# Last dense layer: a chunk of one node tile first, then six of four, with the next chunks' node work between the units

## The chip, the cores and the metric

The kernel runs on one core of one Trainium2 chip. The metric is device time in microseconds (us). Engines: PE is TensorE's matrix multiply and PEld its weight load, DVE is VectorE, ACT is ScalarE, POOL is GpSimd, SP is SyncE, which here only issues DMAs.

## The reference, cut to what matters

Two blocks of graph layer and feed-forward layer run over 3125 nodes of 256 features. The change touches the front of the last feed-forward layer, on the output x of the second graph layer:

```python
# second graph layer: weighted sums over edges, a head's sum divided by its denominator
attn = ex / jnp.maximum(denom[dst], 1e-10)
out = jax.ops.segment_sum(h_src * attn[..., None], dst, num_segments=n)
return out.reshape(n, H * D) + bias
...
# last layer, on the normalized x
H = jax.nn.gelu(xf @ W1 + b1, approximate=False)          # 256 -> 1024
probs = jax.nn.softmax((H @ Wg + bg) / TEMP, axis=-1)     # 8 experts
assign = jnp.argmax(probs, axis=-1)
out = sum over e of where(assign == e, probs[:, e] * (H @ Wd[e] + bd[e]), 0)
...
x = x + _L1_ffn_ref(_layernorm(x, axis=-1)[None], ...)[0]
```

## The kernel before

The 3125 nodes are 25 tiles of 128. Most of the 2.4 ms is spent in stages before the one that is changed: planning and ordering the edges, two graph layers, the first feed-forward layer. Stages are blocks of code one behind the other; every engine has an instruction list of its own in each block, engines wait for one another by semaphores, and a block ends for all engines when the last of them, SP among them, is through.

The change is in `hidden1`, the block that makes the hidden units H of the last layer and the gate's logits. The block behind it routes the nodes to experts, and the one behind that (`last_experts`) gathers rows of H from a table in DRAM (`htab`) and multiplies them with each expert's weights.

`hidden1` goes over the tiles in chunks of CT = 4: six of four tiles and then one of one tile, 128 columns wide instead of 512. A chunk c has FC1 = 8 units j = 8c + f of 128 hidden features each. What each engine does:

- DVE, `node(i)` (lines 1898 to 1904): four operations on a tile: sums times reciprocal of the denominator, plus bias, added to x, and the statistics of the row. `norm.variance(c)` (lines 930 to 936) makes the variances of a chunk in seven small operations, one after the other. `normalized(c)` takes the reciprocal of the root and writes the normalized tiles (line 949). `units_back(j)` (line 1918) copies a unit that was transposed back from PSUM into the buffer `hr`.
- PE, `turn(i)` (line 1955): transposes a normalized tile, in two halves, through two PSUM buffers; `hidden(j)` (line 1965): the matrix product of a unit; `turn_units(j)` (line 1975): transposes the unit back, a tile at a time; `gates(r)` (line 1984): the gate's product over four units; `back(c)` (line 1991): the gate's result turned back.
- ACT, `norm.root(c)` (line 941): the square root; `copy_turned(i)` (line 2023): a transposed tile from PSUM to SBUF; `units(j)` (line 2031): the gelu; `flips(c)` (line 2037): the gate's result from PSUM. Sqrt and gelu need different activation tables, so a root between gelus stands between two table loads, which the profile shows as ACT_TABLE_LOAD on the line of the activation they are for.
- SP: at first the layer's weights, then W1's inputs ahead of 8 MB of expert weights `w2`; then for each chunk x and the units to `htab`, half a chunk's units in one DMA (`store_units`, line 1879).

The order is written out by hand. On DVE, all node work of chunks 0 and 1 stands ahead of the first unit; after that, chunk c + 2's nodes stand between chunk c's units. On ACT, the roots of chunks 0 and 1 both stand ahead of the copies of chunk 0's tiles. PE transposes tile f - 3 of chunk c + 1 behind `hidden` of unit f, from f = 3 on. The waits that tie the engines:

- `hidden(j)` waits for all copies of its chunk's tiles and, as its PSUM has two buffers, for the gelu of unit j - 2;
- `turn_units(j)`, which stands behind `hidden(j + 1)`, waits for the gelu of unit j and, having two buffers too, for `units_back(j - 2)`;
- `turn(i)` waits for the normalized tile i and for the copy of tile i - 2;
- PE's first instruction of the block (line 1996) waits for W1, the biases and the gate's weights.

Of the kernel before, what the change touches and what calls it, by code (L numbers as in the profile page):

```python
# [11 lines left out]
P = 128  # L12
# [3 lines left out]
NT = (N + P - 1) // P  # L16
# [14 lines left out]
FC0, FC1 = F0 // P, F1 // P  # L31
# [849 lines left out]
TB = 5  # L881
# [29 lines left out]
class Norm:  # L911

    def __init__(self, a, tag, per=None):
        self.per = per or TB
        self.st = a.sb(f"{tag}_st", [P, NT, 6])
        self.mean, self.var, self.t0 = (a.sb(f"{tag}_{m}", [P, NT]) for m in ("mean", "var", "t0"))
        self.s_var, self.s_std = a.sem(f"{tag}_var"), a.sem(f"{tag}_std")

    def of(self, c):
        return slice(c * self.per, min(c * self.per + self.per, NT))

# [896 lines left out]
CT = 4  # L1820
CTURNS = (NT + CT - 1) // CT


def hidden1(nc, a, cst, A, x, acc, front):
# [18 lines left out]
    p_g, p_l = a.ps("p_g", [P, 512]), a.ps("p_l", [P, 512])  # L1843
    norm = Norm(a, "norm", CT)
    s_chain, s_in, s_b1, s_bt, s_n, s_t, s_xt, s_h, s_ht, s_g, s_flip, s_l = (a.sem(m) for m in (
# [4 lines left out]
    def tiles(c):  # L1850
        return range(c * CT, min(c * CT + CT, NT))

    def wide(c):
        return len(tiles(c)) * P

    with nc.Block() as block:

        @block.sync
        def _(sp):
# [22 lines left out]
            store_x(0)  # L1882
            store_x(1)
            for c in range(CTURNS):
                store_units(2 * c)
                store_units(2 * c + 1)
                if c + 2 < CTURNS:
                    store_x(c + 2)
            sp.wait_ge(s_store, 16 * CTURNS)
# [4 lines left out]
        def _(dve):  # L1894
# [31 lines left out]
            dve.wait_ge(s_bi, 16)  # L1926
            for c in two:
                for i in tiles(c):
                    node(i)
                norm.variance(link, V, c)  # L1930
                normalized(c)
            for j in range(CTURNS * FC1):
                c, f = j // FC1, j % FC1
                units_back(j)
                if c + 2 < CTURNS:
                    if f < len(tiles(c + 2)):
                        node(tiles(c + 2)[f])
                    if f == CT:
                        norm.variance(link, V, c + 2)
                    if f == CT + 2:  # L1940
                        normalized(c + 2)
            dve.wait_ge(s_in, 64)
            dve.wait_ge(s_l, CTURNS)
# [3 lines left out]
        def _(pe):  # L1947
            T = nc.tensor

            def turn(i):  # L1950
# [3 lines left out]
                for k in range(KC):  # L1954
                    last = T.transpose(p_t[i % 2][:, k * P:(k + 1) * P], n[i // CT % 2][:, i % CT, k * P:(k + 1) * P],
                                       cst["ident"][:])
# [42 lines left out]
            for j in range(CTURNS * FC1):  # L1999
                c, f = j // FC1, j % FC1  # L2000
                hidden(j)
                if c + 1 < CTURNS and f >= 3 and f - 3 < len(tiles(c + 1)):
                    turn(tiles(c + 1)[f - 3])
                if j:
                    turn_units(j - 1)
                if j and j % WAYS == 0:
                    gates(j // WAYS - 1)
                if c and f == 2:
                    back(c - 1)
# [5 lines left out]
        def _(act):  # L2015
            S = nc.scalar

            def copy_turned(i):
                c, b = i // CT, i % CT
                act.wait_ge(s_t, i + 1)  # L2020
# [21 lines left out]
            norm.root(act, S, 0)  # L2042
            norm.root(act, S, 1)
            for i in tiles(0):
                copy_turned(i)
            for j in range(CTURNS * FC1):
                c, f = j // FC1, j % FC1
                units(j)
                if c and f == 0:
                    flips(c - 1)  # L2050
                if f == CT + 2 and c + 2 < CTURNS:
                    norm.root(act, S, c + 2)
                if c + 1 < CTURNS and f >= 3 and f - 3 < len(tiles(c + 1)):
                    copy_turned(tiles(c + 1)[f - 3])
            flips(CTURNS - 1)
# [465 lines left out]
```

## Time and profile before

| | us |
|---|---|
| median of 3 runs | 2420.26 (2420.16, 2420.26, 2425.25) |
| span of the profiled execution, first to last instruction | 2421.0 |
| PE busy, whole span | 1785.6 (74%) |
| DVE busy, whole span | 1638.0 (68%) |
| ACT busy, whole span | 805.9 (33%) |
| `hidden1` in the span, about | 2076 to 2243 |

The profiled execution's own time is known by its span alone; the span is 0.7 us above the median of the runs. A busy share over the whole span says little about one block; the rows further down are from `hidden1` alone, but for two, and their times count from the span's start.

### The profile page before, as it was taken

To read this page: it belongs to the slowest core of one execution; us is meant where nothing else is said; L and a number is where in the kernel's file an instruction comes from. 1 tells how busy PE (TensorE), PEld (TensorE's weight loads), DVE (VectorE), ACT (ScalarE), POOL (GpSimd) and SP (SyncE) were. 2 spreads that over 40 slices of the span, in tenths; PEclk is the share of its full clock that TensorE was granted. 3 is DMA by queue.
4 is the path that set the end of the run, shared out by engine and by line. 5 is a ranking of instruction groups with operands and counts; after the bars stand their busy time and mean duration, and the time that the engine had idled before them with its cause. 6 is when DMAs were issued, how large, how long until landed. Compare 5 with 4: busy or idle time off the path is not lost. (4 is left out here: it accounts for less than half of the span.)

```text
span 2421.0 us, 41392 instructions
## 1 busy us (share of the span) xinstructions
PE 1785.6 (74%) x11452; PEld 1386.4 (57%) x11452; DVE 1638.0 (68%) x3379; ACT 805.9 (33%) x2077; POOL 1152.8 (48%) x1106
## 2 busy tenths in 40 slices
PE   3466666655179996399992878888887887499598
PEld 1245445544057775299991546666665665255587
DVE  8655565555167778655556849999999999764443
ACT  7433333322000002333331644444444444244221
POOL 0277777777700000055550057777777776000243
PEclk9677887887589999599996889999999999799799
DMA  3355555544388862522225145555555553533353
GB/s 86 110 190 192 188 189 173 172 167 165 128 298 284 294 216 103 200 64 73 71 68 180 39 146 146 145 150 142 151 152 145 145 144 113 194 131 119 123 180 104
DMA packets 203758, 368.03 MB, mean 152 GB/s; under 512 B 63193, under 2 KB 111162, under 8 KB 203159
## 3 DMA queue, kind: packets, MB, share of 16 engines
q1 hardware_dynamic: 148066, 205.99, 26.2%
q0 software_dynamic: 54624, 159.35, 21.3%
q8 instruction: 106, 1.74, 0.3%
q14 instruction: 112, 0.92, 0.1%
q10 hardware_dynamic: 850, 0.04, 0.0%
HBM read 235.32 MB, written 130.87 MB: 151 GB/s over the span
## 5 line engine op out<-in xcount | busy, mean ns | idle before, releaser
L2136 POOL DMA_INDIRECT att_rows<-hdram,top_ix x440 | 502.8, 1143 | 264.0 <-issue 133.8
L874 POOL DMA_INDIRECT mtab<-first_w,msgs_ix x280 | 277.5, 991 | 85.3 <-issue 81.1
L1177 POOL IOTA route_spare<- 128x65 f32 (+1 forms) x2 | 0.4, 177 | 522.3 <-POOLq L1115 522.3
L2217 PE MATMUL att_p_acc<-att_msg,att_hot 128*128 128x264 f32 x880 | 225.8, 401 | 14.7 <-DVE wts_wn L2396 6.5
L736 PE MATMUL msgs_p_m<-nodes_n,msgs_hott 128*128 x592 | 185.1, 467 | 48.8 <-issue 30.7
L2251 ACT ACTIVATE att_enc<-att_p_z 128x1024 f32<-128x1024 f32 x110 | 112.7, 1024 | 308.8 <-PE att_p_z L2157 308.8
L2217 PEld LDWEIGHTS att_p_acc<-att_msg,att_hot 128*128 128x128 f32 x880 | 163.4, 196 | 53.2 <-issue 26.6
L874 POOL DMA_INDIRECT mtab<-msgs_rw,msgs_ix x160 | 160.6, 1004 | 68.9 <-issue 44.8
L2166 PE MATMUL att_p_h<-heads_parts,att_hz 128*128 x1320 | 184.3, 295 | 1.4 <-DVE att_enc L2323 1.4
L637 DVE TENSOR_TENSOR first_w<-msgs_p_m,msgs_sorted 128x1024 f32<-128x1024 f32 x70 | 85.6, 1223 | 140.3 <-PE msgs_p_m L736 113.1
L736 PEld LDWEIGHTS msgs_p_m<-nodes_n,msgs_hott 128*128 128x128 f32 x592 | 132.4, 235 | 76.7 <-issue 56.0
L2166 PEld LDWEIGHTS att_p_h<-heads_parts,att_hz 128*128 128x128 bf16 x1320 | 138.2, 105 | 55.0 <-issue 18.2
L2323 DVE TENSOR_TENSOR att_enc<-att_enc,att_p_h 128x1024 f32<-128x1024 f32 x110 | 133.7, 1215 | 20.6 <-PE att_p_h L2166 20.5
L772 PE MATMUL msgs_p_m<-first_w,msgs_hott 128*128 128x256 f32 x616 | 143.2, 385 | 1.2 <-issue 0.3
L2379 DVE TENSOR_TENSOR att_msg<-att_rows,att_ex 128x1024 f32<-128x1024 f32 x110 | 134.7, 1225 | 3.7
L2325 DVE TENSOR_REDUCE att_al<-att_enc 128x32 f32<-128x1024 f32 x110 | 134.2, 1220 | 3.8
L2157 PE MATMUL att_p_z<-top_ewz,att_hz 128*128 128x512 bf16 x220 | 70.5, 403 | 82.7 <-issue 78.5
L1371 PEld LDWEIGHTS exp_hidden<-exp_xt,exp_own 128*128 128x128 f32 x1040 | 127.8, 194 | 4.5 <-issue 1.2
L772 PE MATMUL msgs_p_m<-msgs_rw,msgs_hott 128*128 128x256 f32 x360 | 86.7, 394 | 58.4 <-issue 58.0
L772 PEld LDWEIGHTS msgs_p_m<-first_w,msgs_hott 128*128 128x128 f32 x616 | 110.9, 189 | 32.3 <-issue 17.2
L1371 PE MATMUL exp_hidden<-exp_xt,exp_own 128*128 128x128 f32 x1040 | 128.3, 277 | 1.0 <-DVE exp_own L1317 1.0
L1381 PE MATMUL exp_y<-exp_own,exp_ht 128*128 128x256 f32 x520 | 123.1, 380 | 0.9 <-issue 0.9
(408 smaller groups left out, 3811.7 us busy)
## 6 DMA issues: line engine op xcount, KB each, us to landing
first_w<-mtab SPq DMA_DIRECT2D x77, 520.0 KB, 4.6
etab<-msgs_et SPq DMA_DIRECT2D x110, 288.0 KB, 2.5
att_hz<-etab SPq DMA_DIRECT2D x110, 288.0 KB, 2.9
msgs_rw<-mtab SPq DMA_DIRECT2D x45, 520.0 KB, 4.7
htab<-hid_hr SPq DMA_DIRECT2D x12, 1024.0 KB, 4.3
first_w<-in_L_ffn_w SPq DMA_DIRECT2D x16, 512.0 KB, 5.0
ffn0x_w<-in_L_ffn_w SPq DMA_DIRECT2D x16, 512.0 KB
ffn_w<-in_L_ffn_Wd SPq DMA_DIRECT2D x8, 1024.0 KB
```

The costliest lines, as they stand in the source:

```text
L736: last = T.matmul(p_m[g % 2][:, q, :], hott[g % AHEAD][:, q, :], node[q // UQ], start=True, stop=True)
L772: last = T.matmul(p_m[g % 2][:, 0, :], hott[g % 2][:, q, :], rw[g % RS][:, q, 0:C], start=(q == 0), stop=(q == G - 1))
L874: nc.gpsimd.indirect_dma_start(mtab, bass.IndirectOffsetOnAxis(ap=ix[:, g, q:q + 1], axis=0), rw[g % RS][:, q, :], None).then_inc(s_free[g ...
L1371: last = T.matmul(hidden[t % 2][:, f * P:(f + 1) * P], own1[:, k, f * P:(f + 1) * P], xt[t % 2][:, k * P:(k + 1) * P], start=(k == 0), sto ...
L1381: last = T.matmul(y[t % 2][:, 0:C], ht[t % 2][:, f, :], own2[:, f, :], start=(f == 0), stop=(f == FC - 1))
L2136: nc.gpsimd.indirect_dma_start(rows[:, g % RS, q, :], None, hdram, bass.IndirectOffsetOnAxis(ap=ix1[:, g, q:q + 1], axis=0)).then_inc(s_ro ...
L2166: last = T.matmul(p_h[:, q, :], hott_of(g, q), own[g][q // UQ][:, k, H:HN], start=(k == 0), stop=(k == 2))
L2217: last = T.matmul(p_acc[u % 2][:, 0:HW], hot[g % 2][:, q, :], msg[g % 2][:, q, :], start=(r == 0), stop=(r == UQ - 1))
L2251: S.activation(enc[g % 2][:], p_z[:], ACT.Relu).then_inc(s_enc, 1)
L2323: V.tensor_tensor(e[:], e[:], p_h[:], ALU.mult).then_inc(s_prod, 1)
L2325: V.tensor_reduce(al[t % 2][:, j * G:(j + 1) * G, :].rearrange("p q h -> p (q h)"), e[:].rearrange("p q (h d) -> p (q h) d", h=H), AX, ALU ...
L2379: V.tensor_tensor(msg[g % 2][:].rearrange("p q (h d) -> p q h d", d=D + 1)[:, :, :, 0:D], rows[:, g % RS, :, 0:C].rearrange("p q (h d) -> ...
```

## The change

- The chunks are now bounded by `LEAD` = 0, 1, 5, 9, ..., 25: first one of one tile, then six of four. `Norm` takes these bounds.
- DVE: ahead of the first unit stands only tile 0's node work. Chunk 1's four nodes stand behind units 0 to 3 of chunk 0, its variance behind unit 3, its normalization behind unit 4. Behind every unit of chunk 1 stands a node of chunk 2 or, from unit 4, of chunk 3; chunk 2's variance behind unit 3 and its normalization behind unit 4; chunk 3's variance behind unit 7, its normalization behind unit 1 of chunk 2. From chunk 2 on, as before.
- ACT: `root(1)` and `root(2)` behind the fifth gelu (f = 4) of chunks 0 and 1, `root(3)` behind the second gelu of chunk 2.
- PE: chunk 1's four tiles are transposed behind unit 7 of chunk 0; chunk 2's tiles two and two behind `hidden` of units 6 and 7 of chunk 1; later ones as before.
- SP: x of chunk c + 1, not c + 2, is stored behind chunk c's units; only chunk 0's x ahead of them.

```diff
-    def __init__(self, a, tag, per=None):
-        self.per = per or TB
+    def __init__(self, a, tag, per=None, starts=None):
+        per = per or TB
+        self.starts = starts or [*range(0, NT, per), NT]
...
-        return slice(c * self.per, min(c * self.per + self.per, NT))
+        return slice(self.starts[c], self.starts[c + 1])
...
-CTURNS = (NT + CT - 1) // CT
+LEAD = [0, *range((NT - 1) % CT + 1, NT + 1, CT)]
+CTURNS = len(LEAD) - 1
...
-    norm = Norm(a, "norm", CT)
+    norm = Norm(a, "norm", starts=LEAD)
+    chunk_of = [c for c in range(CTURNS) for _ in range(LEAD[c + 1] - LEAD[c])]
...
-        return range(c * CT, min(c * CT + CT, NT))
+        return range(LEAD[c], LEAD[c + 1])
...
+    def turned_at(c, f):
+        if c + 1 == CTURNS:
+            return ()
+        if c == 0:
+            return tiles(1) if f == FC1 - 1 else ()
+        if c == 1:
+            return {FC1 - 2: tiles(2)[:CT // 2], FC1 - 1: tiles(2)[CT // 2:]}.get(f, ())
+        return tiles(c + 1)[f - 3:f - 2] if f >= 3 else ()
...
             store_x(0)
-            store_x(1)
             for c in range(CTURNS):
                 store_units(2 * c)
                 store_units(2 * c + 1)
-                if c + 2 < CTURNS:
-                    store_x(c + 2)
+                if c + 1 < CTURNS:
+                    store_x(c + 1)
...
-            for c in two:
-                for i in tiles(c):
-                    node(i)
-                norm.variance(link, V, c)
-                normalized(c)
+            for i in tiles(0):
+                node(i)
+            norm.variance(link, V, 0)
+            normalized(0)
             for j in range(CTURNS * FC1):
                 c, f = j // FC1, j % FC1
                 units_back(j)
-                if c + 2 < CTURNS:
+                if c < 2:
+                    if f < CT:
+                        node(tiles(c + 1)[f])
+                    elif c == 1:
+                        node(tiles(c + 2)[f - CT])
+                    if f == CT - 1:
+                        norm.variance(link, V, c + 1)
+                    if f == CT:
+                        normalized(c + 1)
+                    if c == 1 and f == FC1 - 1:
+                        norm.variance(link, V, c + 2)
+                elif c + 2 < CTURNS:
...
+                if c == 2 and f == 1:
+                    normalized(c + 1)
...
                 hidden(j)
-                if c + 1 < CTURNS and f >= 3 and f - 3 < len(tiles(c + 1)):
-                    turn(tiles(c + 1)[f - 3])
+                if c:
+                    for i in turned_at(c, f):
+                        turn(i)
                 if j:
                     turn_units(j - 1)
                 if j and j % WAYS == 0:
                     gates(j // WAYS - 1)
+                if c == 0:
+                    for i in turned_at(c, f):
+                        turn(i)
...
             norm.root(act, S, 0)
-            norm.root(act, S, 1)
             for i in tiles(0):
                 copy_turned(i)
...
-                if f == CT + 2 and c + 2 < CTURNS:
+                if c < 2 and f == CT:
+                    norm.root(act, S, c + 1)
+                if c == 2 and f == 1:
+                    norm.root(act, S, c + 1)
+                if c >= 2 and f == CT + 2 and c + 2 < CTURNS:
                     norm.root(act, S, c + 2)
-                if c + 1 < CTURNS and f >= 3 and f - 3 < len(tiles(c + 1)):
-                    copy_turned(tiles(c + 1)[f - 3])
+                for i in turned_at(c, f):
+                    copy_turned(i)
```

## Rows read from the trace of the kernel before

**Rows 1.** Windows: length; busy us of PE, PEld, DVE, ACT, POOL; clock; DMA share, GB/s.

```profile
2076.00:2103.00 27.00, 2.82 (x10) 1.95 (x11) 21.47 (x63) 3.55 (x9) 0.00 (x0) 0.52 0.97 323
...
2125.00:2232.00 107.00, 106.91 (x475) 55.50 (x474) 58.59 (x143) 46.81 (x76) 0.00 (x0) 1.00 0.33 120
```

**Rows 2.** Timeline, first 30 us: start, us, engine, line, operation [idle before].

```profile
2085.34 0.24 PE L1996 MATMUL hid_p_l<-top_ident,hid_flat 8*128 8x8 f32 x1 [11.78 <-DMA hid_bg<-in_L_ffn_bg]
...
2088.68 1.28 ACT L941 ACT_TABLE_LOAD   x1 [2.90 <-DVE hid_norm_var L936]
...
2100.47 0.20 ACT L941 ACTIVATE hid_norm_t<-hid_norm_var 128x4 f32<-128x4 f32 x1 [10.29 <-DVE hid_norm_var L936]
...
2101.07 1.09 PE L1955 MATMUL hid_p_t<-top_ident,hid_n 128*128 128x128 f32 x4 [9.07 <-ACT hid_xt L2023]
...
2101.77 0.80 ACT L2023 COPY hid_xt<-hid_p_t 128x256 f32<-128x256 f32 x2 [0.57 <-PE hid_p_t L1955]
...
2102.62 6.35 PE L1965 MATMUL hid_p_h<-hid_xt,hid_w 128*128 128x512 f32 x8 [0.46 <-ACT hid_xt L2023]
...
2106.44 0.69 ACT L2031 ACTIVATE hid_ht<-hid_p_h,hid_b1t 128x512 f32<-128x512 f32 x1 [2.57 <-PE hid_p_h L1965]
```

**Rows 3.** Timeline of DVE in the first wide chunk: units with nodes, variance, normalization.

```profile
2109.45 0.69 DVE L1918 COPY hid_hr<-hid_p_r 128x512 f32<-128x512 f32 x1 [7.15 <-PE hid_p_r L1975]
...
2111.89 0.69 DVE L1918 COPY hid_hr<-hid_p_r 128x512 f32<-128x512 f32 x1
...
2120.60 0.15 DVE L930 TENSOR_TENSOR hid_norm_mean<-hid_norm_st 128x4 f32<-128x4 f32 x1
...
2121.79 0.16 DVE L936 SCALAR_TENSOR_TENSOR hid_norm_var<-hid_norm_var,hid_norm_t 128x4 f32<-128x4 f32 x1
...
2125.26 1.38 DVE L949 TENSOR_SCALAR hid_n<-top_x,hid_norm_mean,hid_norm_t 128x256 f32<-128x256 f32 x4
```

**Rows 4.** Timeline of PE: first unit of the second chunk, fourth unit, last wide unit.

```profile
2124.25 1.89 PE L1965 MATMUL hid_p_h<-hid_xt,hid_w 128*128 128x512 f32 x4
...
2132.97 1.96 PE L1965 MATMUL hid_p_h<-hid_xt,hid_w 128*128 128x512 f32 x4
...
2229.64 1.88 PE L1965 MATMUL hid_p_h<-hid_xt,hid_w 128*128 128x512 f32 x4
```

**Rows 5.** Timeline, end of the block: narrow units, gate, first operation behind the block.

```profile
2232.45 0.37 ACT L2031 ACTIVATE hid_ht<-hid_p_h,hid_b1t 128x128 f32<-128x128 f32 x1 [0.20 <-PE hid_p_h L1965]
...
2232.99 0.69 DVE L1918 COPY hid_hr<-hid_p_r 128x512 f32<-128x512 f32 x1 [0.30 <-PE hid_p_r L1975]
...
2240.57 0.29 DVE L1918 COPY hid_hr<-hid_p_r 128x128 f32<-128x128 f32 x1 [0.39 <-PE hid_p_r L1975]
...
2241.28 0.39 PE L1991 MATMUL hid_p_l<-hid_pick,hid_flip 128*128 128x8 f32 x2 [0.39 <-ACT hid_flip L2037]
...
2243.52 0.17 DVE L1120 TENSOR_SCALAR gate_rev<-top_iota 128x8 f32<-128x8 f32 x1 [1.38 <-PEq L1856]
```

**Rows 6.** Waits of SP's queue: who waited for whom: us, times, longest.

```profile
SPq L1891 <- DMA htab<-hid_hr: 1.7, 1, 1.7
```

**Rows 7.** DMA issues of the block: operation, count, KB each, median us to landing.

```profile
htab<-hid_hr SPq DMA_DIRECT2D x12, 1024.0 KB, 4.3
```

**Rows 8.** Timeline of ACT: table loads and their waits, an earlier block and this one.

```profile
1285.49 1.28 ACT L941 ACT_TABLE_LOAD   x1
1303.78 0.21 ACT L941 ACTIVATE upd_norm_t<-upd_norm_var 128x5 f32<-128x5 f32 x1 [17.00 <-DVE upd_norm_var L936]
...
2122.34 1.28 ACT L941 ACT_TABLE_LOAD   x1
...
2124.12 1.28 ACT L2031 ACT_TABLE_LOAD   x1
```

**Rows 9.** Windows: the clock's rise at the start, its fall behind the block.

```profile
2105.00:2110.00 5.00, 5.00 (x12) 2.20 (x11) 0.55 (x1) 1.37 (x2) 0.00 (x0) 0.70 1.04 389
...
2244.00:2246.00 2.00, 0.00 (x0) 0.00 (x0) 1.73 (x6) 0.83 (x2) 0.00 (x0) 0.63 0.01 4
```

More of the change, by code:

```diff
@@ L1954, in turn @@
                 for k in range(KC):
-                    last = T.transpose(p_t[i % 2][:, k * P:(k + 1) * P], n[i // CT % 2][:, i % CT, k * P:(k + 1) * P],
+                    last = T.transpose(p_t[i % 2][:, k * P:(k + 1) * P], n[chunk_of[i] % 2][:, i - LEAD[chunk_of[i]], k * P:(k + 1) * P],
                                        cst["ident"][:])
@@ L2018, in copy_turned @@
             def copy_turned(i):
-                c, b = i // CT, i % CT
+                c, b = chunk_of[i], i - LEAD[chunk_of[i]]
                 act.wait_ge(s_t, i + 1)
```

## The prediction

> **What bounds the kernel now.** The chain that ended last holds only the final store, so it says nothing of this block. The windows by stretch do. Up to 2103 PE works 2.8 of 27 us while DVE works 21.5: a head bound by DVE. From 2125 to 2232 PE is busy 106.9 of 107 us, so PE alone sets the pace of the wide chunks [rows 1]. The timeline of the head shows why it lasts: ACT's second root waited 10.3 us for chunk 1's variance, and the copies of chunk 0's tiles, queued behind it, held PE back until the first `hidden` at 2102.62 [rows 2]. At the other end the last matmul is over at 2241.67, the last unit's copy at 2240.86; SP then waits 1.7 us for the last store to land, and the next block's first DVE operation stands at 2243.52 [rows 5, 6]. So the store of the last units ends the block. From the start of the last wide `hidden`, 2229.64, to this release are 13.88 us [rows 4, 5]. The change shortens the head's first wait, and in exchange puts DVE's nodes on PE's way in chunks 0 and 1. So I sum four places: when the first wide `hidden` starts, what chunks 1 and 2 lose against before's wide chunks, and the tail.
>
> **First narrow unit.** Three nodes fewer stand ahead of chunk 0's variance, so that is no longer last: ACT comes free at 2085.78 (2088.68 less its idle 2.90), behind the loads that PE awaited until 2085.34 [rows 2]. From there: table load 1.28, root 0.2, reciprocal and first normalization 0.6 (a quarter of 1.38, and two short steps), transposes to copy 0.73, copy 0.4 [rows 2, 3]: `hidden(0)` at 2089.2, 13.4 us before its like.
>
> **Chunk 0.** The clock is at half there: a wide `hidden` took 3.4 us plus 0.4 to its gelu (2102.62 to 2106.44), a narrow one then a quarter, 0.85, plus 0.4 [rows 2]. With gelu 0.37 [rows 5] and 0.5 for the transposes back, DVE starts at 2091.35. Here PE, ACT and DVE don't share equally: a wide unit with its node took DVE 2.44 us, without idle between [rows 3]; a narrow copy is 0.40 shorter (0.29 for 0.69 [rows 5]), so 2.04. Four of them and the variance, 1.35 from its first to the end of its seventh operation [rows 3], end at 2100.9. Behind it hang ACT's root and, behind that in ACT's list, the table load and gelu 5, and PE behind gelu 5.
>
> Is the load for the root also on this chain? In an earlier block the load stands right behind ACT's last work, 17 us before its variance came [rows 8]; at 2088.68 it stood behind its variance [rows 2]. In the code the first root waits for one semaphore, the other for two; the moved roots wait for one, so I take the first and keep 1.28 for the range. Then: root 0.25, load 1.28, gelu 0.37, `turn_units(5)` and `hidden(7)` 1.5, gelu 7 0.37 (2104.7). Chunk 1's four tiles now pass two PSUM buffers one behind the other; the last copy ends 2.2 later (0.73 and 0.4 a pair, begun while gelu 7 ran). First wide `hidden`: 2106.9, so **4.3 us later** than before (2102.62). The 13.4 us won are spent.
>
> **Chunk 1.** PE idles from about 2097 to 2102.9, so I start it at half clock. Before, the clock rose at 2108.0 (0.70 as the mean of 2105 to 2110 [rows 9]), 6.9 us after the transposes at 2101.07 [rows 2]; about as long from 2102.9 is 3.0 us into chunk 1. Counted from its first `hidden`: that takes 3.2, narrow transposes and gate 0.45, the second `hidden` 1.7, transposes and hop 0.65: first copy back at 6.0. A node stands behind every unit, so DVE's list in this chunk sums to 8 x 2.44 + 2 x 1.35 + 1.6 = 23.8 [rows 3], against the 21.6 that PE took for a wide chunk. Four units, variance, one more unit with its node, reciprocal and first normalization: 9.76 + 1.35 + 2.44 + 0.6 bring the first tile of chunk 2 at 20.2. PE got there at about 17.3 (five units from 5.35 on, at 1.7 for a product, half of the 3.4 above, and a sixteenth of that, 0.11, for each of the four transposes, with a gate's 1.0 and hops 0.3), and stands 2.9 us. `root(2)` with its load back is over by 18.7 and is hidden behind this. Then two transposes, `turn_units`, `hidden`, two more and `turn_units` (3.6), and 0.75 until the last two copies, which stand behind gelu 7: 24.55. Before's first wide chunk took 2124.25 - 2102.62 = 21.63, half clock included [rows 2, 4]: **2.9 us lost**.
>
> **Chunk 2.** Chunk 1's last unit reaches DVE behind chunk 2's first `hidden`, at 24.55 + 1.7 + 0.65 = 26.9; with its node and chunk 3's variance DVE is through at 30.7. Two units with nodes, 4.88, and 0.6 bring chunk 3's first tile at 36.2. PE wants it behind its fourth `hidden`, 24.55 + 8.72 + 1.7 = 35.0 (8.72 from 2124.25 to 2132.97 [rows 4]): **1.2 us lost**, with 0.3 and 2 as ends. Its pair of loads is hidden as it is in unit 6 of every wide chunk now.
>
> **Nothing for the rest.** The number of roots among wide chunks is as before, five; PE's list there has one transposed tile less, 0.24. SP's stores of x moved behind units wait for tiles long done, and `store_units` behind them go out when their copies end; the expert weights' queue only delays the first of them, whose buffer is wanted again 20 us later.
>
> **Tail.** The last chunk is wide. Last `hidden` to the end of its copy: 2233.68 - 2229.64 = 4.04 [rows 4, 5]; its store is 1 MB, 4.3 to landing [rows 7]; release 0.6 later (2243.52 less 2240.86, less the wait of 1.7 and about 0.4 for the issue): 8.94 instead of 13.88, **4.94 us won**. The gate's end, by 6.6, is covered by the store; were the store as quick as the last one was, the gate would end the block and 2 us more be won.
>
> **Sum.** 4.3 + 2.9 + 1.2 - 0.24 - 4.94 = +3.2 us. It is made on the profiled execution, whose span, 2421.0, lies 0.7 above the median; I add it to the median: 2423.5.
>
> The Trainium skill (ScalarE: Activation LUTs, What ACT_TABLE_LOAD costs) gives a switch about 1.28 us and as much again of drain, 2.66 in all. Here the load agrees, but between the loads at 2122.34 and 2124.12 only 0.5 us is left for a root and a copy [rows 8], so no drain is seen. By the page the load back in chunk 0 would cost 1.38 more, and the sum be +4.6.
>
> **Rivals.**
> - *Clock up early.* If PE's work on narrow units lets the clock rise before chunk 1, that starts DVE's row 1.4 us sooner and the sum is +1.8, 2422.0. For it: PE works most of the last 4 us ahead. Against: a 5 us idle before.
> - *Clock falls again.* PE's 2.9 us stand in chunk 1 may put it back to half: it fell at 2244.5 (0.63 as mean of 2244 to 2246 [rows 9]), 2.8 us after the last matmul [rows 5]. The next rise costs half of 5.4 us, as 2102.62 to 2108.0 did: +5.9, 2426.2. The Trainium skill (TensorE: Matmul & The Clock Gate, HAM oscillation) has such gaps in a loop put the clock back each time; the fall in the row agrees with it.
> - *The load stands behind its wait*, as at 2088.68: 1.28 more in chunk 0, some 0.5 in chunk 1: +5.0, 2425.3.
> - *A switch costs a second load's 1.28*, in ACT's list where no idle is shown: on the chain once, +4.5, 2424.8.
> - *Faster.* Chunk 1's nodes fit between narrow units. Before, the eight narrow units at the end went through in some 9 us. At that pace the first wide `hidden` is at 2089.2 + 9 + 2.2 = 2100.4, 2.2 sooner than before, and with DVE ahead chunks 1 and 2 lose nothing: -2.2 - 0.24 - 4.94 = -7.4, 2412.9. It decides for faster where the first three terms together are under 0.3. Against it: DVE had no idle between units with nodes [rows 3], and a narrow unit saves it only 0.40.
>
> **How the numbers follow.** Forecast 0.52; clock early 0.17; clock falls 0.17; load behind its wait 0.04; dearer switch 0.03; faster 0.07. 0.2%, about what a measurement of this kernel can tell from no change, is 4.8 us, so the forecast with its spread (2.0 to 4.8) and the early clock lie within it. Slower: the fall 0.17, half of the two small cases, and 0.06 of the forecast's upper end: 0.27. Faster 0.07, the same 0.66. The low end of the range is the early clock with chunk 2's loss at 0.3: +0.9, and a little under it for hops that I priced too high: 2420.5. The high end is the fall with the clock's first rise late too (1.2 more): 2427.5.
>
> **What would show it.** First `hidden` at 2089 and first wide `hidden` at 2106.9 (2100 for the faster rival); in chunk 0 DVE without idle from 2091 to 2101, ACT's root(1) right behind variance 1, its load ahead of it. In chunk 1 PE waiting for DVE's line 949, some 3 us, and again, shorter, in chunk 2. PE idle ahead of the first wide `hidden` while ACT copies. At the end SP's wait for the last store some 4 us, ended by its landing. A first wide `hidden` off by over 2 us, no wait on line 949, or a store that lands in 2 us would make the sum wrong.

## The result and the profile after

The changed kernel took 2433.38 us (median of 20 runs, 2424.87 to 2439.81) beside 2424.91 for the kernel before (20 runs, 2417.36 to 2436.26): a ratio of 1.0036, 95% interval 1.0025 to 1.0047; of 2424.91 that is 8.7 us more, with 6.1 and 11.4 as ends (the two medians themselves lie 8.5 apart). The prediction was 2423.5 with 2427.5 as its upper end. The three runs of before that it was added to had a median of 2420.26, which lies 4.65 below that of the 20.

The profiled execution of the changed kernel has a span of 2438.0, 17.0 more than the one of before. Most of that is not in the block that was changed: its first DVE operation stands at 2089.01 instead of 2076.50. From there to the release of the next block are 170.89 us instead of 167.02, and from the release (the next block's first DVE operation) to the end 178.07 instead of 177.43. Below, the block is also counted from PE's first matmul in it, since what stands ahead of that is the wait for the weights, 7.9 to 9.2 us in the profiles of the two kernels: 161.72 instead of 158.18.

The head and the first two chunks, in the timeline of the changed kernel (start, us, engine, line, operation, idle before):

```profile
2098.18 0.24 PE L2019 MATMUL hid_p_l<-top_ident,hid_flat 8*128 8x8 f32 x1 [12.12 <-DMA hid_bg<-in_L_ffn_bg]
...
2101.99 2.08 PE L1988 MATMUL hid_p_h<-hid_xt,hid_w 128*128 128x128 f32 x8 [0.46 <-ACT hid_xt L2050]
...
2104.32 0.29 DVE L1929 COPY hid_hr<-hid_p_r 128x128 f32<-128x128 f32 x1 [3.54 <-PE hid_p_r L1998]
...
2106.88 1.28 ACT L942 ACT_TABLE_LOAD   x1
...
2113.89 0.21 ACT L942 ACTIVATE hid_norm_t<-hid_norm_var 128x4 f32<-128x4 f32 x1 [5.72 <-DVE hid_norm_var L937]
2114.11 1.28 ACT L2058 ACT_TABLE_LOAD   x1
...
2115.83 0.47 PE L1998 MATMUL hid_p_r<-top_ident,hid_ht 128*128 128x128 f32 x1 [6.19 <-ACT hid_ht L2058]
...
2119.80 1.98 PE L1988 MATMUL hid_p_h<-hid_xt,hid_w 128*128 128x512 f32 x4 [0.46 <-ACT hid_xt L2050]
...
2138.81 0.76 PE L1978 MATMUL hid_p_t<-top_ident,hid_n 128*128 128x128 f32 x4 [2.46 <-DVE hid_n L950]
...
2140.09 3.33 PE L1988 MATMUL hid_p_h<-hid_xt,hid_w 128*128 128x512 f32 x4
...
2144.74 1.98 PE L1988 MATMUL hid_p_h<-hid_xt,hid_w 128*128 128x512 f32 x4 [0.44 <-ACT hid_xt L2050]
...
2156.55 0.44 PE L1978 MATMUL hid_p_t<-top_ident,hid_n 128*128 128x128 f32 x2 [1.28 <-DVE hid_n L950]
```

These answer to [rows 2, 3]. Counted from PE's first matmul (2098.18), the first `hidden` is 3.81 us behind it (17.28 before), the first wide one 21.62 (4.3 later than before). ACT's second root waits 5.72 us for its variance, with its table already loaded; PE stands (sits idle between two pieces of work) 6.19 us for the gelu that is queued behind. In chunk 1, from 2119.80 to 2144.74, PE stands 2.46 us for DVE's normalized tile, and the `hidden` behind this stand takes 3.33 us, the one ahead of it and the others 1.9 to 2.0. In chunk 2 it stands 1.28 us for DVE. The same two chunks as windows (length, busy us of PE, PEld, DVE, ACT, POOL, clock, DMA share, GB/s):

```profile
2119.80:2144.74 24.94, 22.04 (x88) 11.01 (x88) 17.10 (x44) 9.55 (x16) 0.00 (x0) 0.93 0.27 98
2144.74:2167.73 22.99, 21.71 (x96) 11.36 (x97) 18.58 (x51) 10.94 (x18) 0.00 (x0) 1.00 0.32 115
```

The clock was full (2.4 GHz) when chunk 1 began and fell to half (1.2 GHz) in the stand, so that its mean is 0.93; before, it was low at the start of the first wide chunk [rows 9] and full in all later ones [rows 1]. The end of the block, and the wait of SP's queue in it:

```profile
2251.03 1.88 PE L1988 MATMUL hid_p_h<-hid_xt,hid_w 128*128 128x512 f32 x4
...
2255.10 0.36 SPq L1891 DMA_DIRECT2D htab<-hid_hr  x1
...
2259.90 0.17 DVE L1121 TENSOR_SCALAR gate_rev<-top_iota 128x8 f32<-128x8 f32 x1 [2.32 <-PEq L1868]
```

```profile
SPq L1902 <- DMA htab<-hid_hr: 3.8, 1, 3.8
```

Against [rows 5, 6]: the last wide `hidden` starts 8.87 us ahead of the release, not 13.88, and the wait for the last store has grown from 1.7 to 3.8.

### The profile page after: what moved, and what is told of

Read it like the earlier page. It is cut to its first block and busy times, and to the rows that moved or that the text cites. A ratio compares the mean times of both kernels' runs of the same rounds, so it can differ in the third digit from the quotient of the medians.

```text
span 2438.0 us, 41398 instructions
## 1 busy us (share of the span) xinstructions
PE 1796.6 (74%) x11452; PEld 1395.8 (57%) x11452; DVE 1640.4 (67%) x3379; ACT 809.0 (33%) x2079; POOL 1158.1 (48%) x1106
## 5 line engine op out<-in xcount | busy, mean ns | idle before, releaser
L2247 PE MATMUL att_p_acc<-att_msg,att_hot 128*128 128x264 f32 x880 | 231.6, 409 | 13.9 <-DVE att_total L2423 6.5
```

The costliest lines, as they stand in the source:

```text
L2247: last = T.matmul(p_acc[u % 2][:, 0:HW], hot[g % 2][:, q, :], msg[g % 2][:, q, :], start=(r == 0), stop=(r == UQ - 1))
```

## The experiments

**First group: drift or the change?** Three theories stood against each other for the 17 us between the two profiles: (A) the change costs what its block shows, the rest is drift of the stages ahead; (B) the changed program also lengthens the stages ahead; (C) the block itself costs about 8 in most runs.

*The changed kernel, run again.* No edit.

> The changed kernel as it is, timed and profiled once more. Theory A (the change costs what its block shows, about 4 us, and the rest of the 8.5 us is run-to-run drift of the stages ahead): block from PE's first matmul to the next block's first DVE operation 161 to 162.5 us against 158.2 before, and the whole time 3 to 6 us above the kernel before in this job. Theory B (the change also lengthens the stages ahead, by where the program lies): block as in A, the whole time 8 us above or more, and the first matmul of the block again some 8 to 13 us later than before's 2085.3. Theory C (the block itself costs about 8 us in most runs, and the profiled run was lucky with the clock): block 165 us or more.

Measured: 2429.37 (12 runs), ratio 1.0030 [1.0013, 1.0046], which is 7.3 us (3.2 to 11.1): more than A's 3 to 6, less than B's 8, with an interval that holds both. In its profile the block begins at 2073.24, 3.3 us sooner than in the kernel before, and takes 161.79 from the first matmul, as A and B have it. So C falls, and the 12.5 us ahead of the block do not come with the change each time. They did not come from the attention stage alone either: 6.0 of them were there when its first transfer started, first in the kernel before, then in the changed one:

```profile
1408.47 0.32 SPq L2124 DMA_DIRECT2D att_seg<-segtab  x1
```

```profile
1414.47 0.32 SPq L2154 DMA_DIRECT2D att_seg<-segtab  x1
```

A smaller part of B is not excluded. From that transfer to the block's first DVE operation the three full profiles of the changed kernel take 674.5, 669.6 and 671.9 us, those of the kernel before 668.0, 667.9 and, with the padding below, 670.4: 3.2 more on the mean, with ranges that overlap.

*Both kernels without the attention stage:*

```
-                with ExitStack() as c1:
-                    attention(nc, Pool_(nc, c1, "att"), ...
```

> The kernel before without the second graph layer's attention stage, so that the sums keep the values they are started with. That stage is the one whose gathers make times drift. It takes about 690 us of the span, so 1720 to 1740 us is expected by all theories; what tells them apart is its difference to the next kernel.

> The changed kernel without the attention stage, to be compared with the one above. A: 3 to 5 us longer, all of it between the block's first matmul and the next block. B: as much in the block, and 2 us or more in the stages ahead of it. C: about 8 us longer, all in the block.

Measured: 1753.81 and 1760.07 (5 runs each), 6.26 apart. Block 165.25 and 171.16, 5.9 apart, which is nearly all of it. The difference is over A's 3 to 5 and under C's 8. The block begins 6.0 us later in the changed kernel's profile (1410.77 against 1404.80), as B has it, but that profile is of the slowest of its five runs and the other of the fastest, so it settles nothing. That the attention stage is the one that drifts is borne out in part at most: it took 666.1 to 674.5 us in the full profiles, but without it five runs of one kernel still spread over 8.6 us. That its gathers are the cause no run shows.

*The kernel before with a few instructions more* at the end of the block:

```
+            for k in range(4):
+                link(V.memset(pad[:, k:k + 1], 0.0))
...
+            for k in range(2):
+                S.copy(pad[:, 4 + k:5 + k], b1t[:, k:k + 1])
```

> The kernel before with four tiny DVE operations and two tiny ACT copies at the end of the block, as many instructions as the change adds on these engines, where both engines wait. A and C: the same as the kernel before, within 2 us, and the block 158 to 159 us. B: 3 us or more slower, in the stages ahead of the block.

Measured: ratio 0.9998 [0.9982, 1.0013]; block 165.71, from the first matmul 157.32 (expected 158 to 159). These instructions cost nothing that can be told within some 4 us either way, so B's 3 us or more is not seen.

**Second group: the change taken apart.** The first theory of each expectation is the one of the block's own terms.

*The normalization ahead of the node,* in chunks 0 and 1 of the changed kernel:

```
                 if c < 2:
+                    if f == CT:
+                        normalized(c + 1)
                     if f < CT:
                         node(tiles(c + 1)[f])
...
-                    if f == CT:
-                        normalized(c + 1)
```

> The changed kernel, but in chunks 0 and 1 the normalizations of the next chunk stand on DVE ahead of the node behind the fifth unit, not behind it. Theory 1 (chunk 1 is long because PE stands 2.46 us for DVE's first normalization, and because the clock falls in that stand, 3.33 us instead of 1.88 for the hidden behind it): the node took 1.7 us of that path, so PE's stand in chunk 1 is about 0.7 us, the clock stays up, chunk 1 takes 22 to 23 us instead of 24.93, the first wide hidden starts some 0.5 us earlier or as before, and the kernel is 2 to 3 us faster than the changed one: ratio about 1.002 to the kernel before. Rival (the clock falls for another reason than this stand, or DVE's row as a whole is the bound): chunk 1 stays at 24 to 25 us and the ratio at 1.003 to 1.004.

Measured: 2423.74, ratio 1.0006 [0.9994, 1.0018]. PE's timeline:

```profile
2102.76 3.78 PE L1988 MATMUL hid_p_h<-hid_xt,hid_w 128*128 128x512 f32 x4 [0.46 <-ACT hid_xt L2050]
...
2121.84 0.76 PE L1978 MATMUL hid_p_t<-top_ident,hid_n 128*128 128x128 f32 x4 [0.62 <-DVE hid_n L950]
...
2123.43 1.88 PE L1988 MATMUL hid_p_h<-hid_xt,hid_w 128*128 128x512 f32 x4
```

The stand is 0.62 as expected and the `hidden` behind it takes 1.88: no fall. But here the clock was still at half when chunk 1 began (3.78 for its first `hidden`), so the chunk lasts 23.86 us, not 22 to 23. The median is better than expected (1.5 us over before, -1.5 to 4.4), the block, 170.27, worse: one profile of a kernel does not stand for its runs where the clock is in play, and the attention stage took 666.1 us in this one, less than in any other.

*Only the chunk bounds,* with the order of the kernel before (cut to the bounds themselves):

```
-CTURNS = (NT + CT - 1) // CT
+LEAD = [0, *range((NT - 1) % CT + 1, NT + 1, CT)]
+CTURNS = len(LEAD) - 1
```

> Only the chunk bounds are changed (1 tile and six times 4), the order of the work is that of the kernel before. Theory 1 (the loss in chunks 1 and 2 comes from the nodes between the units, the gain at the end from the wide last chunk): chunks 1 and 2 lose nothing against a wide chunk but the late rise of the clock, the tail still takes 8.9 us, and the last stage is as in the kernel before. The first hidden waits for chunk 1's nodes and stands some 13 us behind the first matmul, the first wide hidden some 23.5 us, 2 us later than in the changed kernel: block 168 to 169 us, total 1 to 3 us over the kernel before. Rival (the narrow chunk itself makes the losses): chunk 1 takes 24 us and more here too, the block 171 us or more, total 5 us over or more.

Measured: 2424.11, ratio 1.0009 [0.9998, 1.0020]; block 168.96. Timeline of ACT and PE:

```profile
2095.23 0.21 ACT L942 ACTIVATE hid_norm_t<-hid_norm_var 128x4 f32<-128x4 f32 x1 [9.32 <-DVE hid_norm_var L937]
...
2095.75 2.07 PE L1968 MATMUL hid_p_h<-hid_xt,hid_w 128*128 128x128 f32 x8 [8.45 <-ACT hid_xt L2026]
...
2106.66 0.30 PE L1978 MATMUL hid_p_r<-top_ident,hid_ht 128*128 128x128 f32 x1 [1.23 <-DVE hid_hr L1921]
...
2108.35 3.78 PE L1968 MATMUL hid_p_h<-hid_xt,hid_w 128*128 128x512 f32 x4 [1.40 <-ACT hid_xt L2026]
```

The root of chunk 1 holds the head for 9.32 us, as before, and narrow units wait for DVE: the first wide `hidden` comes 24.40 behind the first matmul. The chunk behind takes 22.72 (clock at half at first), the next 21.65, a wide chunk's time, and the last `hidden` starts 9.00 ahead of the release. So the losses of chunks 1 and 2 come from the new order, and the gain at the end from the bounds. That it is the nodes in this order rather than the root or the transposes rests on PE's waits for DVE and on the swap above, which took 1.84 us off the stand by moving one node.

*Only the nodes and the root between the units* (and the transposes that hang on them), with the bounds of the kernel before:

```
-            for c in two:
+            for i in tiles(0):
+                node(i)
...
+                if c < 1:
+                    if f < CT:
+                        node(tiles(c + 1)[f])
+                    else:
+                        node(tiles(c + 2)[f - CT])
...
-            norm.root(act, S, 1)
...
+                if c < 1 and f == CT:
+                    norm.root(act, S, c + 1)
```

> Bounds as in the kernel before (six times 4 and 1); only the nodes, variance, normalizations and root of chunk 1 stand between the units of chunk 0, as the changed kernel has them in its chunk 1. Theory 1 (the nodes between the units cost what they push back: about 3 us in the first chunk and 1.3 in the next, but let the first hidden start some 9 us sooner): first hidden at 8 us behind the first matmul instead of 17, chunk 0 24 to 25.5 us instead of 21.6, the chunk behind it 1.3 longer, total 3 to 5 us faster than the kernel before. Rival (wherever nodes stand between units, the first chunk runs at half clock and stands for DVE, and the gain at the head is spent again): total within 2 us of the kernel before.

Measured: 2419.34, ratio 0.9980 [0.9964, 0.9995]. PE's timeline:

```profile
2092.35 5.83 PE L1986 MATMUL hid_p_h<-hid_xt,hid_w 128*128 128x512 f32 x8 [0.46 <-ACT hid_xt L2044]
...
2112.80 0.76 PE L1976 MATMUL hid_p_t<-top_ident,hid_n 128*128 128x128 f32 x4 [2.65 <-DVE hid_n L950]
...
2113.93 3.49 PE L1986 MATMUL hid_p_h<-hid_xt,hid_w 128*128 128x512 f32 x4
```

The first `hidden` is 8.59 behind the first matmul, 8.7 sooner than in [rows 2]; the first chunk takes 26.37, not 24 to 25.5, with such a stand (2.65) and such a fall of the clock (3.49) as in the changed kernel. By the runs about half of the 8.7 us is left (4.8, with 1.2 and 8.7 as ends), as theory 1 had it. The profile shows less: the release is 155.57 behind the first matmul, 2.6 sooner than in the first profile of before, and the stage behind it takes 179.8, the longest of all.

*Only ACT's root of chunk 1 moved,* behind the second gelu:

```
             norm.root(act, S, 0)
-            norm.root(act, S, 1)
...
+                if j == 1:
+                    norm.root(act, S, 1)
```

> The kernel before with one thing moved: ACT's root of chunk 1 stands behind the second gelu instead of ahead of the copies of chunk 0's tiles. Theory 1 (the head of the block before was held back by this root's wait of 10.3 us alone): the first hidden starts about 8 us behind the first matmul instead of 17, DVE still does chunk 1's nodes first, and PE stands for the first unit back or not at all: block 6 to 8 us shorter, total 5 to 8 us faster. Rival (DVE's 24 nodes bound the head, whatever the order on ACT): the first wide chunk becomes longer by as much as the head becomes shorter, total within 2 us.

Measured: 2413.63, ratio 0.9969 [0.9952, 0.9986]; block 158.59. Timeline:

```profile
2088.30 6.01 PE L1965 MATMUL hid_p_h<-hid_xt,hid_w 128*128 128x512 f32 x8 [0.46 <-ACT hid_xt L2023]
...
2095.06 1.28 ACT L941 ACT_TABLE_LOAD   x1
...
2096.36 0.20 ACT L941 ACTIVATE hid_norm_t<-hid_norm_var 128x4 f32<-128x4 f32 x1
...
2098.11 0.68 DVE L1918 COPY hid_hr<-hid_p_r 128x512 f32<-128x512 f32 x1
```

The first `hidden` is 7.69 behind the first matmul, and DVE does all nodes of chunk 1 (four, of the eight at the head) while PE transposes and works on the first two wide units, mostly at half clock. The root waits for nothing, PE is busy 21.71 us of this chunk's 22.07, and the release is 149.28 behind the first matmul, 8.1 sooner than on the mean of before's profiles below. In PE's waits of the block's first 50 us the one for a normalized tile is that of the first transposes (us, times, longest):

```profile
PE hid_p_t L1955 <- DVE hid_n L949: 4.7, 1, 4.7
```

**Third group: the clock, and what one profile is worth.**

*The changed kernel with its stands filled* by matmuls that nothing reads:

```
+                for k in range({FC1 - 2: 16, 2 * FC1 - 2: 8}.get(j, 0)):
+                    T.matmul(p_l[:, 256:512], cst["ident"][:], w1[:, 0, 0:256], start=True, stop=True)
```

> The changed kernel, with matmuls that nothing reads put into PE's list where it stands: 16 of 256 columns ahead of the transposes of unit 5 in chunk 0 (PE stands 6.2 us there), 8 ahead of chunk 2's first transposed tile in chunk 1 (2.5 us there). Theory 1 (the stand of 2.46 us in chunk 1 put the clock back to half, and the hidden behind it took 3.33 us instead of 1.88): with the fillers the clock stays up from chunk 0 on, chunk 1's first hidden and the one behind the stand both take 1.9 to 2.0 us, chunk 1 lasts 23.4 us instead of 24.93, and the block is 1.4 us shorter than the changed kernel's 170.9 if the fillers fit into the stands. Rival (the fall has another cause, or DVE's row sets the end of chunk 1 anyway): chunk 1 stays within 0.4 us of 24.9.

Measured: 2427.22, ratio 1.0011 [0.9998, 1.0024]; block 168.41. PE's timeline:

```profile
2099.05 7.07 PE L2026 MATMUL hid_p_l<-hid_w,top_ident 128*128 128x256 f32 x32
...
2108.71 1.98 PE L1988 MATMUL hid_p_h<-hid_xt,hid_w 128*128 128x512 f32 x4 [0.46 <-ACT hid_xt L2052]
...
2125.10 3.62 PE L2026 MATMUL hid_p_l<-hid_w,top_ident 128*128 128x256 f32 x16
2128.55 0.60 PE L1978 MATMUL hid_p_t<-top_ident,hid_n 128*128 128x128 f32 x4
...
2129.43 1.88 PE L1988 MATMUL hid_p_h<-hid_xt,hid_w 128*128 128x512 f32 x4
```

The clock stays full from chunk 0 on: 1.98 for chunk 1's first `hidden`, 1.88 behind the filled stand. That is theory 1; the rival, a chunk within 0.4 us of 24.9, falls. Chunk 1 takes 23.91, not 23.4: from the start of the `hidden` ahead of the stand to the transposes are 5.17 us (2123.38 to 2128.55), where the profile of the changed kernel has 4.34 (2134.47 to 2138.81), so the second filler was 0.8 too long. Without that 0.8 it would be 23.1. So I estimate the fall's share of the changed kernel's chunk 1 at 24.94 less 23.1, some 1.8 us, of which the one `hidden` shows 1.45 (3.33 less 1.88).

*Both kernels again, unchanged, on one chip.*

> The changed kernel itself, on one chip with the kernel before. Theory 1 (block 5 us longer than the kernel before on the mean of its profiles, of which the 167.0 us of the first profile is the upper end; the stage behind it longer or shorter by the time at which the clock rises in it): block 170.9 us, ratio 1.002 to 1.0035. Rival (the stage behind the block is longer by the change itself): it takes 178 us or more from the block's release here too, against 177.4 or less for the kernel before, and the clock rises 33 us or more behind the release.

> The kernel before itself, once more under its own profile. Theory 1 (what its block takes depends on when the clock rises in its first wide chunk, and what the stage behind it takes on when it rises there, by chance): block between 165 and 167 us, the stage behind it anywhere from 176.8 to 179. Rival (the stage behind the block is longer in the changed kernel by the change itself): that stage takes 177.4 us or less here, with the clock up by 32 us behind the release.

Measured: 2429.16, ratio 1.0020 [1.0007, 1.0033], for the changed kernel; 0.9997 [0.9986, 1.0007] for the kernel before. Blocks 169.07 (not 170.9) and 165.25. PE in the changed kernel:

```profile
2110.07 3.13 PE L1988 MATMUL hid_p_h<-hid_xt,hid_w 128*128 128x512 f32 x4 [0.46 <-ACT hid_xt L2050]
...
2130.21 0.76 PE L1978 MATMUL hid_p_t<-top_ident,hid_n 128*128 128x128 f32 x4 [2.44 <-DVE hid_n L950]
...
2131.24 1.88 PE L1988 MATMUL hid_p_h<-hid_xt,hid_w 128*128 128x512 f32 x4
```

This time the clock is low at chunk 1's start and does not fall in the stand, which is as long as it was (2.44). PE in the kernel before, which answers to [rows 2, 4]:

```profile
2083.11 0.24 PE L1996 MATMUL hid_p_l<-top_ident,hid_flat 8*128 8x8 f32 x1 [11.08 <-DMA hid_bg<-in_L_ffn_bg]
...
2100.90 4.76 PE L1965 MATMUL hid_p_h<-hid_xt,hid_w 128*128 128x512 f32 x8 [0.46 <-ACT hid_xt L2023]
...
2120.94 1.89 PE L1965 MATMUL hid_p_h<-hid_xt,hid_w 128*128 128x512 f32 x4
```

Its first two `hidden` take 4.76 us, where the first profile has 6.35, and its first wide chunk 20.04 instead of 21.63. Behind the block, windows of the stage with the experts' products: first the kernel before in its first profile (release at 2243.52), then in this one (release at 2240.22):

```profile
2265.00:2273.00 8.00, 3.66 (x16) 3.26 (x17) 1.75 (x2) 1.71 (x3) 5.65 (x5) 0.50 0.88 277
2273.00:2277.00 4.00, 4.00 (x16) 3.32 (x15) 0.00 (x0) 0.63 (x2) 0.00 (x0) 0.72 1.00 402
```

```profile
2270.00:2274.00 4.00, 4.00 (x13) 3.35 (x12) 0.00 (x0) 1.17 (x2) 0.00 (x0) 0.53 0.96 396
2274.00:2278.00 4.00, 4.00 (x24) 3.58 (x23) 1.92 (x3) 1.08 (x2) 0.08 (x1) 1.00 0.04 15
```

In the first the clock rises in the window that begins 29.5 us behind the release and has 0.72 as its mean; in the second the window 29.8 behind it has 0.53. By these means it rises 31.7 and 33.5 us behind the release (worked out as the point that splits the window between 0.5 and 1), and the rest takes 177.43 and 178.86 us. So the kernel before, too, can have the longer last stage that I had seen in the profiles of the changed one (178.07 to 178.55), and its length goes with the time of the rise: in before's other two profiles it is 30.6 and 31.5, with 176.78 and 177.05. The rival does not fall altogether: in all four profiles of the changed kernel the rise comes 33.3 to 33.5 behind the release, in one of four of the kernel before. With so few, whether the change makes the late rise likelier stays open.

*No chunk of one tile, and the root moved:* chunks of 3, 4, 4, 4, 4, 3 and 3 tiles.

```
+LEAD = [0, 3, 7, 11, 15, 19, 22, 25]
...
-            norm.root(act, S, 1)
...
+                if j == 1:
+                    norm.root(act, S, 1)
```

> The kernel before with chunk 1's root moved behind the second gelu, as in the last call, and no chunk of one tile: the chunks hold 3, 4, 4, 4, 4, 3 and 3 tiles. Theory 1 (the head was held back by that root's place in ACT's list, the end by a chunk too small to feed PE; DVE's work ahead of the first unit costs nothing while PE is busy with wide units): first hidden some 5.5 us behind the first matmul, release some 147 us behind it, instead of 149.3 with the root alone moved and 158 before; block 156 to 157 us, ratio 0.995 to 0.997. Rival (chunks of 3 make DVE or ACT the bound, as their fixed costs a unit weigh more): the chunks of 3 take more than 17 us each, against 16.2 for three quarters of a wide one, and the release is no sooner than with the root alone moved.

Measured: 2415.02 (5 runs), ratio 0.9966 [0.9953, 0.9979]; block 159.56. The first `hidden` is at 5.43 as expected, but the release at 150.25, not 147:

```profile
2098.22 0.52 PE L1978 MATMUL hid_p_r<-top_ident,hid_ht 128*128 128x128 f32 x3 [1.09 <-DVE hid_hr L1921]
...
2109.11 1.99 PE L1968 MATMUL hid_p_h<-hid_xt,hid_w 128*128 128x512 f32 x4 [1.16 <-ACT hid_xt L2026]
```

The chunks of 3 take 20.22 at the start, where waits of PE for DVE and ACT of some 3 us come in between, and 17.42 later. That is the rival's outcome; its reason holds at the start only, since later PE itself is busy 17.01 of the 17.42 us, more than the 16.2 of three quarters of a wide chunk. It is no better than the root alone moved, which is one line; that is the version to keep.

## Why the prediction was wrong

All profiles of the two kernels side by side, in us; "first matmul" is PE's first of the block, the release is the next block's first DVE operation. Of before: the first profile, without attention, with the padding, and run again; of after: the first, again, without attention, and again.

| | before | mean | after | mean |
|---|---|---|---|---|
| first matmul to first wide `hidden` | 17.28, 16.23, 17.57, 17.79 | 17.22 | 21.62, 21.71, 20.42, 21.69 | 21.36 |
| first wide chunk | 21.63, 21.34, 20.48, 20.04 | 20.87 | 24.94, 24.92, 27.32, 24.38 | 25.39 |
| second wide chunk | 21.65, 21.64, 21.64, 21.64 | 21.64 | 23.00, 23.01, 23.00, 22.98 | 23.00 |
| first matmul to release | 158.18, 156.80, 157.32, 157.11 | 157.35 | 161.72, 161.79, 162.86, 161.22 | 161.90 |
| release to end | 177.43, 177.05, 176.78, 178.86 | 177.53 | 178.07, 178.46, 178.55, 178.44 | 178.38 |

The step that failed has two parts: the base to which the sum was added, and the sum's term for chunk 1. A third part of the miss lies outside the block and stays open. None of the signs that the prediction named for a wrong sum came.

- **First narrow unit, and chunk 0: right.** First `hidden` 3.81 behind the first matmul (3.86 by the prediction), first wide one 4.3 later than before in the pair, 4.1 on the means. The order was as described: the load ahead of its wait, DVE without a stop from its first unit to the variance, PE 6.19 behind gelu 5. So "faster" fell here, and "load behind its wait" too. The dearer table switch fell as well: the root at 2113.89 took 0.21, the load back stood at 2114.11 and took 1.28, with nothing between, so no drain either. The prediction has the clock at half in chunk 0; it rises there in all four profiles and falls again in the stand of 6.2 us. DVE set the pace, so this changed little.
- **Chunk 1: the term that was mis-sized.** The prediction has 24.55 against "Before's first wide chunk took 2124.25 - 2102.62 = 21.63, half clock included": 2.9 lost. Measured 24.94 in the pair, 3.3 lost, and 4.5 lost on the means. Two things were mis-sized. The chunk of before was read from one profile in which the clock rose late; the others have it at 20.04 to 21.34, so that the mean of all is 0.8 less. And the chunk of after is 0.8 longer on the mean, because the two rivals on the clock were weighed as alternatives to the forecast, each alone, when both were live in every run: full at the chunk's start and fallen in the stand (two profiles), low at the start and not fallen (one, 24.38), low and fallen (one, 27.32). The forecast's own case is low at the start and not fallen, and its 24.55 was right to 0.2; but it was given a chance of 0.52 against 0.17 for the fall, and the fall came in three of four (priced at 2.7, it cost some 1.8 by the estimate above). The rise was put 3.0 us into the chunk; it came ahead of the chunk in two profiles and 2.3 and 5.1 us into it in the others. PE's stand itself was 2.46, 2.44, 2.44 and 2.44 where the prediction had 2.9: DVE's tile came when it said (20.14 for 20.2 in the profile of that case), but PE reached the stand 0.4 later, as a product took it 1.88 to 1.98, the 1.89 of [rows 4], and not 1.7.
- **Chunk 2, the rest of the block, the tail: right.** 1.36 lost (1.2), by a second stand of 1.28; the last wide `hidden` to release 8.87 (8.94), with the wait for the last store of 3.8 ("some 4"); the wide chunks between them 0.45 shorter (0.24).
- **The sum** on the means is 4.14 + 4.52 + 1.36 - 0.45 - 5.01 = 4.56, against a measured difference from the first matmul to the release of 4.55, where the prediction had 3.2. So the block's excess over the prediction is chunk 1's 1.6, less 0.3 in the other terms.
- **The base: wrong, and the largest part.** "I add it to the median" took three runs whose median was 2420.26; medians of 20 to 35 runs were 2423.26 to 2424.91. Beside the 2424.91 of the result this is 4.65 of the 9.9 us between forecast and result. The block's sum is 1.35 of them, and 3.9 lie outside the block in this comparison, to which the prediction gave nothing. The range, whose ends were all made of the block's own costs, had no room for either.
- **What the runs say of the whole.** The changed kernel was measured three times against the kernel before, side by side: 8.7 [6.1, 11.4], 7.3 [3.2, 11.1] and 4.8 [1.7, 8.0] us, and 6.3 between the short pair. The profiles explain 4.6 in the block, and 5.4 with the last stage's 0.85 counted, which may be chance. All three intervals hold 6.1 to 8.0; what lies between that and the profiles, 0.7 us at the least, stays open. The 3.2 us by which the attention stage is longer on the mean would cover it, but whether the change has a part in it no run here shows: the start of the block lies between 2073.24 and 2089.01 in three profiles of the same changed kernel.

The change gave 5.0 us at the end by its bounds, and lost that and more at the head. The first `hidden` came 13.5 us sooner, since the root of chunk 1 no longer stood in ACT's list ahead of work that was ready and only one tile's node ahead of it on DVE; but the nodes and the same root then stood between narrow units, so that chunk 0 took 17.8 us, and between wide ones in chunk 1, and cost all of it and more. The root alone, moved to another place in ACT's list, is worth 7.5 us (3.4 to 11.6).

The Trainium skill (TensorE: Matmul & The Clock Gate, HAM oscillation) has waits of some 3 to 5 us in a loop put the clock back each time. The stand of 2.9 that the prediction counted among such gaps is at the short end of that, and those measured are shorter still. Of the five stands of 2.44 to 2.65 us in a wide chunk that these profiles show, four put it back (3.31 to 3.52 for the `hidden` behind them, 1.88 otherwise) and one did not; the one of 0.62 and those of 1.28 did not either.

## What to carry to other kernels

Where an engine's list holds a wait ahead of work that is ready, move that one instruction first and measure, before the work that feeds it is moved: here DVE's nodes held PE up by under 0.4 us beside wide units at work (21.71 of 22.07 us busy), and, with the root and its table load behind them, for 6.2 us between narrow ones. The base of a forecast needs as many runs as the result will have: three gave a median 4.65 us under that of twenty. A term that is the difference to a stage "before" needs more than one profile of it when the clock rises in that stage, since the rise alone moved it by 1.6 us. Where a stand can put the clock back, its price belongs into the forecast together with the stand, not beside it as another case.

## What was not expected of the hardware

The same instructions of the block with the same stand of 2.44 to 2.46 us on PE kept the full clock in one profile and lost it in three others. In the kernel before the first wide chunk took between 20.04 and 21.63 us, and the last stage between 176.78 and 178.86, the longer the later the clock rose in them. The block began up to 15.8 us apart in profiles of one and the same kernel, about twice what the change costs, and 10.8 of these were there ahead of the attention stage.
